# Masked keys of layer 1 replaced by their batch's mean key, and the token tiles without their mask rows

## The reference, cut to what matters

```python
q = (x @ Wq).reshape(B, N, HEADS, hd).transpose(0, 2, 1, 3)
k = (context @ Wk).reshape(B, M, HEADS, hd).transpose(0, 2, 1, 3)
v = (context @ Wv).reshape(B, M, HEADS, hd).transpose(0, 2, 1, 3)
scores = jnp.einsum('bhid,bhjd->bhij', q, k) * scale
max_neg = -jnp.finfo(scores.dtype).max
scores = jnp.where(context_mask[:, None, None, :], scores, max_neg)
attn = jax.nn.softmax(scores, axis=-1)
out = jnp.einsum('bhij,bhjd->bhid', attn, v)
...
x = x + _L0_xattn_ref(_layernorm(x, axis=-1), ctx_768, ...)
x = x + _L0_ffn_ref(_layernorm(x, axis=-1), ...)
x = x + _L1_xattn_ref(_layernorm(x, axis=-1), ctx_768, mask_BxS2_bf1, ...)
x = x + _L1_ffn_ref(_layernorm(x, axis=-1), ...)
```

## Time and profile before

| | |
|---|---|
| Three runs | 293.08, 293.55, 295.0 us; median 293.55 us |
| Profiled execution | 294.46 us, span 292.7 us from first to last instruction |
| Busy in the span | PE 265.0 us (91%), PEld 189.3 (65%), DVE 205.5 (70%), ACT 203.7 (70%), POOL 101.6 (35%) |
| Mean granted TensorE clock | 0.983 |

### The profile page before, as it was taken

How to read it: one execution, slowest core, us unless ns; L and a number is a source line. 1 busy time by engine, 2 the same in 40 slices (tenths; PEclk the granted TensorE clock), 3 DMA queues, 4 the chain that set the end, 5 groups by cost and what they waited for, 6 DMA issues and landing times.

```text
span 292.7 us, 5757 instructions
## 1 busy us (share of the span) xinstructions
PE 265.0 (91%) x2075; PEld 189.3 (65%) x2075; DVE 205.5 (70%) x535; ACT 203.7 (70%) x303; POOL 101.6 (35%) x119
## 2 busy tenths in 40 slices
PE   8898989899998528888899999999999999999993
PEld 8776454655676217755545677776678578788872
DVE  3898776945996896799945886692548457745764
ACT  4735766188529837312677967898999996957991
POOL 3791996068950500120111000460202702107180
PEclk9999999999999995899999999999999999999999
DMA  7537000000000000000000000000000000000001
GB/s 232 164 85 212 1 2 3 0 2 0 2 1 2 0 0 0 2 0 1 2 3 2 0 2 0 2 0 3 0 36 3 0 0 2 0 37 2 0 1 72
DMA packets 4573, 6.45 MB, mean 22 GB/s; under 512 B 1181, under 2 KB 2898, under 8 KB 4546
## 3 DMA queue, kind: packets, MB, share of 16 engines
q1 hardware_dynamic: 3426, 3.47, 3.8%
q0 software_dynamic: 848, 2.35, 2.8%
q10 hardware_dynamic: 272, 0.27, 0.3%
HBM read 5.04 MB, written 1.05 MB: 21 GB/s over the span
## 4 chain that ended last, share of the span: by engine, by line
PE 53%; DVE 5%; ACT 2%; issue 2%; POOL 1%; DVEq 0%; POOLq 0%
PE ps L1107 6%; PE ps L1096 6%; PE ps L1109 5%; PE ps L1097 5%; PE ps L1098 5%; PE ps L1108 5%; PE ps L1006 3%; PE ps L988 2%; PE ps L947 2%; PE ps L968 1%; PE ps L1014 1%; PE ps L1042 1%; PE ps L1085 1%; DVE mxr L697 1%; ACT p L501 1%
## 5 line engine op out<-in xcount | busy, mean ns | idle before, releaser
L779 DVE TENSOR_TENSOR hhl<-hf,hhl 128x512 fp32r<-128x512 f32 x64 | 42.7, 689 | 26.7 <-ACT hf L571 24.0
L501 ACT ACTIVATE p<-ps 117x1024 f32<-117x1024 f32 (+1 forms) x48 | 46.2, 1021 | 15.1 <-PE ps L998 15.0
L697 DVE TENSOR_REDUCE mxr<-ps 128x8 f32<-128x616 f32 x64 | 47.6, 793 | 12.2 <-PE ps L978 12.0
L570 ACT ACTIVATE hhl<-ps,b 128x512 fp32r<-128x512 f32 x64 | 45.9, 717 | 10.4 <-PE ps L1109 6.0
L571 ACT ACTIVATE hf<-ps,b 128x512 f32<-128x512 f32 x64 | 46.0, 718 | 0.0
L888 PE MATMUL ps<-ones 128*128 128x128 f32 x230 | 36.8, 308 | 1.5 <-POOL ones L387 1.0
L888 PEld LDWEIGHTS ps<-ones 128*128 128x128 f32 x230 | 33.5, 219 | 6.5 <-issue 2.9
L344 POOL TENSOR_SCALAR veps<-mv 128x4 f32<-128x4 f32 x16 | 5.2, 327 | 81.8 <-DVE mv L627 81.6
L444 POOL TENSOR_TENSOR lq<-ebase,lg 128x32 f32<-128x32 f32 x4 | 22.3, 5587 | 19.0 <-DVE lg L818 18.9
L1107 PE MATMUL ps<-hhl,w2l 128*128 128x512 f32 x64 | 26.8, 419 | 0.0
L1096 PE MATMUL ps<-x1buf,w1l 128*128 128x512 f32 x64 | 26.4, 413 | 0.0
(11 more groups left out here) (188 smaller groups left out, 565.5 us busy)
## 6 DMA issues: line engine op xcount, KB each, us to landing
x<-in_x SPq DMA_DIRECT2D x4, 256.0 KB, 4.5
w1raw<-in_w POOLq DMA_DIRECT2D x1, 1024.0 KB, 6.3
w2raw<-in_w POOLq DMA_DIRECT2D x1, 1024.0 KB, 7.2
out<-xn SPq DMA_DIRECT2D x4, 256.0 KB, 2.1
ctxw<-in_ctxw SPq DMA_DIRECT2D x1, 280.0 KB, 5.1
kmo<-in_kmo POOLq DMA_DIRECT2D x1, 220.0 KB, 8.0
ctxw<-in_ctxw ACTq DMA_DIRECT2D x1, 192.5 KB, 3.5
wqo<-in_wqo SPq DMA_DIRECT2D x1, 192.0 KB, 5.6
```

The costliest lines, as they stand in the source:

```text
L501: act.activation(p[0:w, j, 2 * half:2 * half + 2, :], pair_of("key", u, j, half)[0:w], ACT.Exp, scale=SCALE).then_inc(q["p_ready"], 1)
L570: act.activation(hh[:, b % HR, :], bank_of("w1", 1, b), ACT.Gelu, bias=b1[:, b % NH:b % NH + 1])
L697: nc.vector.tensor_reduce(mxr[:, u % 2, j, 2 * half:2 * half + 2, :], heads[:, :, :, 0:M], AX.X, ALU.max).then_inc(q["tok_maxed"], 1)
L779: nc.vector.tensor_tensor(hl[:, b % HR, :], hf[:, b % HF, :], hh[:, b % HR, :].bitcast(F32), ALU.subtract).then_inc(q["h_lo"], 1)
```

## The change

The mask leaves the token tiles. DVE's `keys_masked` gets six more instructions: the sum of the unmasked keys and their count for each batch, the count limited to 1 from above (`kany`) and from below, the reciprocal, and the mean key (`kmean`); `k_masked` is announced after the last of them. POOL's `keys_widened` puts the mean at masked positions (three more instructions on 128x312), and `mask_rows` multiplies the mask row by `kany` (one more). A mean of unmasked keys has a score no higher than the highest unmasked one, so the maximum stays what it was. PE's token tiles of layer 1 lose the four matmuls of L975, and the wait for `kmx_set` moves to the key tiles. The constant `kmo` loses its 128 columns `one8`, so its load shrinks.

```diff
-        kmo = sb("kmo", [128, KR + 128], F32R)
-        kmx0, one8 = kmo[:, 0:KR], kmo[:, KR:KR + 128]
+        kmx0 = sb("kmo", [128, KR], F32R)
...
             def keys_widened():
                 pool.wait_ge(q["k_masked"], 1)
+                fill = klo.bitcast(F32).rearrange("p (b j) -> p b j", b=B)
+                done(nc.gpsimd.tensor_scalar(fill, cmask[:, :, :], -1.0, 1.0, ALU.mult, ALU.add), "pool_self")
+                done(nc.gpsimd.tensor_tensor(fill, fill, kmean[:, :].unsqueeze(2).broadcast_to([128, B, MP]), ALU.mult), "pool_self")
+                done(nc.gpsimd.tensor_tensor(kf[:, :], kf[:, :], klo.bitcast(F32), ALU.add), "pool_self")
                 done(nc.gpsimd.tensor_copy(khi, kf[:, :]), "pool_self")
...
                 done(nc.gpsimd.tensor_scalar(kf[:, :], cmask[:, :, :].rearrange("p b j -> p (b j)"), -1.0, sel, ALU.add, ALU.mult), "pool_self")
+                rows = kf[:, :].rearrange("p (b j) -> p b j", b=B)
+                done(nc.gpsimd.tensor_tensor(rows, rows, kany[:, :].unsqueeze(2).broadcast_to([128, B, MP]), ALU.mult), "pool_self")
...
-                    pool.dma_start(kmo[:, :], a["kmo"].bitcast(F32R)).then_inc(q["kmo_in"], 16)
+                    pool.dma_start(kmx0[:, :], a["kmo"].bitcast(F32R)).then_inc(q["kmo_in"], 16)
...
-                nc.vector.tensor_tensor(kf[:, :], src, cmask[:, :, :].rearrange("p b j -> p (b j)"), ALU.mult).then_inc(q["k_masked"], 1)
+                link(nc.vector.tensor_tensor(kf[:, :], src, cmask[:, :, :].rearrange("p b j -> p (b j)"), ALU.mult))
+                nc.vector.tensor_reduce(kmean[:, :], kf[:, :].rearrange("p (b j) -> p b j", b=B), AX.X, ALU.add)
+                link(nc.vector.tensor_reduce(kcount[:, :], cmask[:, :, :], AX.X, ALU.add))
+                nc.vector.tensor_scalar(kany[:, :], kcount[:, :], 1.0, None, ALU.min)
+                link(nc.vector.tensor_scalar(kcount[:, :], kcount[:, :], 1.0, None, ALU.max))
+                link(nc.vector.reciprocal(kcount[:, :], kcount[:, :]))
+                nc.vector.tensor_tensor(kmean[:, :], kmean[:, :], kcount[:, :], ALU.mult).then_inc(q["k_masked"], 1)
...
                         pe.wait_ge(q["k_split_pool" if L else "k_split"], 1)
-                        if L == 1:
-                            pe.wait_ge(q["kmx_set"], 1)
...
-                        if L == 1:
-                            for r in range(R):
-                                rows = slice(32 * r, 32 * r + 32)
-                                mm(banks[r][:, 0:KR], one8[rows, :], kmx1[rows, b, :], start=False, stop=False)
...
                         pe.wait_ge(q["mt_copied"], u + 1)
                         pe.wait_ge(q["kmo_in"], 16)
+                        if L == 1:
+                            pe.wait_ge(q["kmx_set"], 1)
```

More of the change, by code:

```diff
@@ L180, in build @@
         kbd = sb("kbd", [128, 2, 2, B, KR], F32R)
-        kmo = sb("kmo", [128, KR + 128], F32R)
-        kmx0, one8 = kmo[:, 0:KR], kmo[:, KR:KR + 128]
+        kmx0 = sb("kmo", [128, KR], F32R)
         kmx1 = sb("kmx1", [128, B, KR], F32R)
         kf = sb("kf", [128, B * MP])
+        kmean = sb("kmean", [128, B])
+        kcount = sb("kcount", [128, B])
+        kany = sb("kany", [128, B])
         khl = sb("khl", [128, 2, B * MP], F32R)
@@ L1163, in shape_constants @@
                 vmask[0:w, c, :, sums] += here[:, None]
-    kmo = np.zeros((128, KR + 128), np.float32)
+    kmo = np.zeros((128, KR), np.float32)
     for h in range(HR4):
@@ L1168, in shape_constants @@
             kmo[d % 32 == 2 * h + s, MP * h:MP * h + M] = -1.0
-    kmo[d % 32 == MASKROW, KR:] = 1.0
     return cst, vmask.reshape(PR, NC * D), kmo
```

## The result

| | before | after |
|---|---|---|
| Median of 12 runs each, same chip | 293.62 us (293.08 to 295.0) | 297.08 us (295.25 to 298.63) |
| Profiled execution, its span | 294.46, 292.7 us | 297.09, 295.2 us |
| Mean granted TensorE clock | 0.983 | 0.977 |

The ratio is 1.0100, 95% interval 1.0078 to 1.0123, or +2.3 to +3.6 us; it is not that of the two medians, which differ by 3.46 us. The forecast was 293.7 us with a range up to 295.4; the rival nearest to the result is the one by the clock.

The account below looks back on a forecast made before the run. PE was taken to bound layer 1, with PE and DVE handing tiles over nearly without slack in layer 0's attention. -1.4 + 1.6 + 0 + 0 = +0.2 us on the 293.55 median gave 293.7 us, range 292.2 to 295.4.

Parts of the forecast that it names:

- slower by the clock: Layer 0, PE's pause before tok.0.2: if long enough, the clock halves behind it, +4.4 us, 298.1 us; chance 0.04.
- The row of 2.8 us at full clock: Profile before: the clock was granted in full through 2.8 us holding 0.11 us of PE work.
- part 2: Layer 0 attention: six added DVE instructions delay PE's tok.0.2 by 1.67 us; +1.6 us, bounds +1.3 and +2.6.
- Part 1: Layer 1 token tiles: removed matmuls save 0.14 us a round where not hidden; -1.4 us, bounds -0.9 and -2.2.
- only the loss shows: Layer 1: ACT proves the true pacer, PE only waits more, 0.1 to 0.3 of the gain left; 295.0 us; chance 0.12.
- the change does nothing: Whole kernel: the removed round was hidden in all tiles and the additions are too; 293.5 us; chance 0.02.
- the 0.9 of its rival: Layer 0, added short DVE instructions: held up beside POOL's DMA issues, +0.9 us, 294.6 us; chance 0.10.
- Passes undiminished: Layer 0 to layer 1: the delay from the added DVE instructions reaches layer 1 whole, +1.6 us.
- early work absorbed: Layer 0: idle time of DVE and PE between 27 and 60 us absorbs the added work; 292.1 us; chance 0.10.
- Part 3: POOL's added instructions in `keys_widened` and `mask_rows`: hidden or within slack; 0, bounds 0 and +0.4 us.
- the conditions that I named: Wrong if layer 1's first tile moves under 1 or over 2.5 us, PE gaps after 160, or clock falls before 100.

Follow-up runs that it names:

- with three reductions: Kernel before with three reductions of 312 elements, read by nobody, between DVE's mask product and `k_masked`: ratio 1.0081 (1.0046 to 1.0117).
- the filled pause: Changed kernel with 8 matmuls on ones, read by nobody, ahead of layer 0 tok.0.2's wait for `k_masked`: ratio 1.0022 against the kernel before, 294.83 us.
- the kernel with 17 filling matmuls: Changed kernel with 17 matmuls on ones, read by nobody, ahead of layer 0 tok.0.2's wait for `k_masked`: ratio 1.0064 against the kernel before, 296.08 us.
- The kernel without `kany`: Changed kernel without POOL's product with `kany` in `mask_rows`: ratio 1.0072 (1.0043 to 1.0100) against the kernel before.

## Why the prediction was wrong

**The step that failed is the rival "slower by the clock".** It named the mechanism, the place and the sign, and then set aside all but 0.04 of its chance with one sentence: "It decides from a pause between 2.8 and 5.3 us". These bounds came from two pauses elsewhere. I carried them over to a place with other work around it. At this place a pause of 1.34 us left the clock at 1.00 and pauses of 1.71, 1.85 and 2.19 us were followed by 0.50. The row of 2.8 us at full clock was true of the one trace that I had, and still no lower bound, not even for its own place: all fourteen kernels of this study have this pause of 2.7 us, and in eleven of their profiles the clock fell between 0.6 us before its end and 1.9 us after it. Windows of after, where the pause ends at 103.79:

```profile
103.00:105.00 2.00, 1.21 (x3) 0.38 (x3) 1.97 (x5) 1.11 (x3) 1.00 (x1) 0.72 0.00 0
105.00:107.00 2.00, 2.00 (x8) 1.47 (x8) 1.97 (x3) 1.65 (x3) 0.85 (x1) 0.50 0.00 0
```

The length of the new pause was misread too. The rival has PE stand still from 17.8 to 19.3 us; by the prediction's own rows it is the old 0.22 us and the 1.67 us of part 2, so 1.9 us, and 2.19 were measured.

Its price was mis-sized the other way: +4.4 us, from a low stretch of 8.8 us behind the 5.28 us pause. Here the clock stayed low for 6.8 us in the profile of after (by one-microsecond windows, from 18.5 to 25.4 us; the shown window of 6.25 us at 0.50 is the part with PE at work), which cost 2.75 us, and for 3.4 us with three reductions, which cost 1.66. By the filled pause it was 2.3 us in the median.

**Part 1** predicted -1.4 us; measured -1.42 alone and -1.75 in the whole. The late tiles gave 33.89 - 32.91 = 0.98 us over seven tiles from tok.2.0 to tok.3.3, which is the 0.14 us a round that was read from the trace. The rival *only the loss shows* falls with it, and *the change does nothing*.

**Part 2** predicted 1.67 us for PE's start; measured 1.88. The reductions were right; the difference of 0.2 us is the hold of the two limits beside POOL's DMA issue, 0.3 us and not the 0.9 of its rival, less 0.1 us that the links and the reciprocal took under their prices. "Passes undiminished" was right: in the kernel with the pause filled the first key tile was 13.72 us behind tok.0.0, +1.72. The rival *early work absorbed* falls. What the step lacked is that PE's delay is not only a delay: the same 1.9 us of standing still changes how fast it runs afterwards.

**Part 3** predicted 0, bounds 0 to +0.4; measured +0.42. I had expected the shift to free the first small instruction and the wait for POOL's 1/sqrt to take its place. In fact the first stayed held for part of its time and the third was held for 0.95 us.

With the measured terms and a full clock the sum is -1.42 + 1.88 + 0.42 = +0.9 us, or 294.4, inside the range; the run with the pause filled gave +0.65. The clock's 2.3 us took it out. The range of the sum alone, 292.9 to 294.6, was stated narrower than its bounds allow: with both parts at their ends they give 292.65 to 295.25.

Of the conditions that I named, layer 1's first tile at 131.18 had moved by 4.25 us (over 2.5), and the clock fell ahead of 100 us. Both fired; the third, gaps after 160 us, did not.

## What to carry to other kernels

Where a change puts time into a hand-over between two engines that run closely in turn, price PE's pause twice: once as a delay, and once as the clock behind it, and do not take a pause that one trace shows at full clock for a bound: that of 2.7 us kept it in three profiles of fourteen. Test it cheaply: a few matmuls that nobody reads in the pause, or a dose of useless work at that place, tell a clock effect from a delay in one run each. And before accepting a trade of late gain for early cost, look for a slot where the engine waits anyway: the same six instructions cost 1.9 us and a clock stretch at 17 us, and nothing that shows at 43 us.

## What the runs showed of the hardware that was new to me

- **At one place the clock's answer to a pause was a step in the profiles, and it is not the same for the same pause.** 0.81 and 1.34 us: nothing. 1.71 to 2.19 us, in five kernels: half clock. Yet the pause of 2.7 us in layer 0's feed-forward, which ends at 99 us in before, had no such answer in three kernels of fourteen and had it in the other eleven. The time at which it fell was not fixed to the pause either: by one-microsecond windows it fell some 0.5 us ahead of the pause's end in the changed kernel, and with three reductions some 0.7 us after PE had resumed. What makes the cases differ was not tried.
- **What a low stretch costs depends on who waits there.** The one at 103 to 109 us in after cost nothing: from the first to the second global maximum the fourteen kernels took 21.49 to 21.51 us, with and without it. One at 33 to 37 us, in the kernel with 17 filling matmuls, goes with 63.49 us from the first key tile to the first global maximum, where four kernels with the same code in that stretch, after among them, took 62.28 or 62.29: 1.2 us that no edit explains. The kernel without `kany` had one at the same place. What sets them off stays open; a single profile can be off by one.
- **DVE's smallest instructions wait out POOL's.** A scaling of 128x2 elements took 0.14 to 0.17 us free, and 1.07 to 1.12 us where a POOL product of 128x512 ran; in each case it ended as that product did. Beside POOL's cast of the same size it took 0.53 to 0.54 us and ended with the cast. The two limits of 128x4 ended within 0.04 us of the end of a POOL DMA issue of 1.00 us, in all six kernels that have them at this place. Not every instruction waits: the reciprocal of 128x2 took 0.17 us while a POOL product ran (85.43 to 85.60; the product started at 85.46), the count's reduction kept its price beside that same issue, and the last product of 128x4 took 0.16 us beside the next one. The Trainium skill (SBUF — State Buffer, Who interferes with whom) states that a `tensor_scalar` in a two-port mode takes a port pair that GpSimd shares, for the whole instruction, and that the later of the two is blocked until the first is done. The traces agree in kind, with a hold of 0.9 to 1.0 us for the product and 0.3 to 0.4 for each limit; in which mode the instructions ran stands in no trace.
